# Global attention: the row step of the score maxima moved one unit earlier, and the results evicted by ScalarE through the score banks and finished on GpSimd

## The reference, cut to what matters

```
h = _layernorm(x) * (1 + ca) + sa
q, k, v = 16 heads of 8 features each, of h            # 4 sequences x 1024 tokens
scores = einsum('bhqd,bhkd->bhqk', q, k) / sqrt(8)
attn = softmax(scores, axis=-1)                        # needs the row maximum and the row sum
out = einsum('bhqk,bhkd->bhqd', attn, v)
x = x + ga * (out @ Wo.T + bo)
```

## Time and profile before

| what | value |
|---|---|
| median of 3 runs | 3825.5 us (3819.56 to 3826.06) |
| profiled execution, its own time | 3821.91 us |
| its span | 3820.1 us |
| PE, DVE, ACT, POOL busy in the span | 96%, 84%, 75%, 63% |
| loop of global attention, first score to last weighing | 87.24 to 748.29 us |
| mean granted PE clock | 0.987 of 2.4 GHz |

### The profile page before, as it was taken

One profiled execution on the slowest core, in us unless ns is written; L12 is line 12 of the kernel. 1 busy time (PEld: TensorE's weight loads), 2 busy tenths in 40 slices (PEclk: granted clock), 3 DMA queues, 4 the chain that ended last, 5 costly groups with the idle time before them and its releaser, 6 DMA issues. The chain is left out here.

```text
span 3820.1 us, 161411 instructions
## 1 busy us (share of the span) xinstructions
PE 3661.5 (96%) x70604; PEld 2660.4 (70%) x70604; DVE 3217.1 (84%) x4678; ACT 2863.7 (75%) x5074; POOL 2397.6 (63%) x1986
## 2 busy tenths in 40 slices
PE   6999999959999999999999999999999999999997
PEld 2222222247888888888888888888888888888885
DVE  7999999668888888888888888888888888888884
ACT  3888888857777777777777777777777777777774
POOL 3100000077777777878777777778777777778783
PEclk8999999989999999999999999999999999999999
DMA  3110000034444344433444344444444443444432
GB/s 117 38 39 21 20 22 18 7 95 109 110 112 106 104 122 113 111 107 104 119 115 112 105 106 116 120 110 105 106 116 116 111 106 105 127 117 109 108 105 57
DMA packets 202568, 360.17 MB, mean 94 GB/s; under 512 B 35522, under 2 KB 74054, under 8 KB 201542
## 3 DMA queue, kind: packets, MB, share of 16 engines
q1 hardware_dynamic: 201802, 348.76, 34.3%
HBM read 236.73 MB, written 111.67 MB: 91 GB/s over the span
## 5 line engine op out<-in xcount | busy, mean ns | idle before, releaser
L1202 POOL TENSOR_TENSOR T<-T 128x1024 f32<-128x1024 f32 x384 | 909.2, 2380 | 25.9 <-DVE T L1681 25.1
L1220 POOL TENSOR_TENSOR T<-T,rn 128x1024 f32<-128x1024 f32 x384 | 732.0, 1907 | 27.1 <-POOL rn L1213 0.4
L1292 PE MATMUL PA<-Wqkv,XS 128*128 128x512 f32 x2304 | 633.4, 410 | 11.4 <-DVE XS L1642 8.2
L787 ACT ACTIVATE E<-p_low 128x512 f32<-128x512 f32 x1024 | 556.2, 597 | 114.6 <-PE p_low L637 100.5
L716 DVE TENSOR_REDUCE negmax<-p_max 128x1 f32<-128x1024 f32 x512 | 588.9, 1215 | 19.7 <-PE p_max L616 19.7
L1292 PEld LDWEIGHTS PA<-Wqkv,XS 128*128 128x128 f32 x2304 | 414.7, 193 | 81.9 <-DVE XS L1642 11.2
L1689 DVE TENSOR_REDUCE ss<-SQ 128x32 f32<-128x2048 f32 x192 | 436.9, 2275 | 0.0
L1368 PE MATMUL PB<-ET,VW 64*64 64x32 f32 x24576 | 399.6, 220 | 16.8 <-DVE T L1681 8.8
L1368 PEld LDWEIGHTS PB<-ET,VW 64*64 64x64 f32 x24576 | 377.5, 135 | 54.8 <-DVE T L1681 28.6
L1320 PE MATMUL PD<-ident,T 128*128 128x128 f32 x3072 | 409.5, 276 | 6.3 <-POOL T L1220 5.3
L1381 PEld LDWEIGHTS PD<-Wo,OT 128*128 128x128 f32 x3072 | 365.9, 192 | 61.3 <-issue 61.1
(11 more groups left out here) (165 smaller groups left out, 6718.8 us busy)
## 6 DMA issues: line engine op xcount, KB each, us to landing
VW<-v_rows SPq DMA_DIRECT2D x768, 256.0 KB, 4.5
v_rows<-Vs SPq DMA_DIRECT2D x192, 512.0 KB, 6.0
Wraw<-in_Wqkv SPq DMA_DIRECT2D x40, 192.0 KB, 5.1
QA<-parts_q SPq DMA_DIRECT2D x384, 16.0 KB
KA<-parts_k SPq DMA_DIRECT2D x192, 32.0 KB
parts_q<-AO SPq DMA_DIRECT2D x8, 384.0 KB, 2.7
parts_k<-AO SPq DMA_DIRECT2D x8, 384.0 KB, 3.3
Wo<-in_Wo SPq DMA_DIRECT2D x12, 256.0 KB, 4.8
```

Of the source, the lines that this page charges most:

```text
L787: act.activation(E[:, s % 4, c, :], p_s[:, (64 * g + i) % NS, :], ACT.Exp, scale=DH ** -0.5)\
L1202: pool.tensor_tensor(out=t_, in0=t_, in1=T2[:, i * HALF:(i + 1) * HALF], op=ALU.add).then_inc(ad.sem, 1)
L1220: pool.tensor_tensor(out=t_, in0=t_, in1=rn[:, p, i * LH:(i + 1) * LH].unsqueeze(2).broadcast_to([P, LH, LD]), op=ALU.mult).then_inc(no.se ...
L1292: mm = pe.matmul(pair[:, half, :], XS[:, b, i, 1:P + 1], Wqkv[:, l % 2, j, lo:lo + 512], start=(k == 0), stop=(k == 2))
```

## The change

The row step moves from step 5 (and 13) to step 4 (and 12). It now stands between the two units of that step, behind the first unit of the next half, and the late order is gone: all steps have the same order. For this the units stand two earlier in the steps, and 8 instead of 6 of the first group's second half are done ahead of the loop. The PE transpose of the row step waits for the 16th unit of its half, two turns back, and no longer for the turn just before it.

The transposed results go to the next bank of the score ring instead of to `p_max`. ACT copies them out of it into `OE`, in its order among the exponentials, and POOL takes the reciprocals (a power of -1) and the products. `ring` numbers scores and results together. ACT's next copy of `p_o` into the same half of `OE` waits for POOL's product (`s_ao`).

```
-        if s < 5:
-            return [(g, 1, 6 + 2 * s + i) for i in range(2)]
+        if s < 4:
+            return [(g, 1, 8 + 2 * s + i) for i in range(2)]
...
-        return [(0, 0, i) for i in range(HU)], [(0, 1, i) for i in range(6)]
+        return [(0, 0, i) for i in range(HU)], [(0, 1, i) for i in range(8)]
...
+    def ring():
+        at = {}
+        def add(kind, *key):
+            at[(kind, *key)] = len(at)
+        for g in range(NG):
+            for s in range(16):
+                add("score", g, s, 0)
...
                 if s == 3 and g > 0:
                     add("result", g - 1, 1)
                 if s == 11:
...
     def on_pool(pool):
+        def result(g, qh):
+            b, hg = divmod(g, HG)
+            o = OE[:, qh, :].rearrange("p (q c w) -> p q c w", q=4, w=VW)
+            pool.wait_ge(s_ex.sem, s_ex.at(RING["result", g, qh]))
+            pool.tensor_tensor(out=rsum[:, qh, :, :], in0=o[:, :, :, DH], in1=minus[:, :, :], op=ALU.pow)\
+                .then_inc(s_rc.sem, 1)
+            pool.wait_ge(s_rc.sem, s_rc.at(g, qh + 1))
...
+            pool.tensor_tensor(out=a[:, :, hg, :, :], in0=o[:, :, :, 0:DH],
+                               in1=rsum[:, qh, :, :].unsqueeze(3).broadcast_to([P, 4, GH, DH]),
+                               op=ALU.mult).then_inc(s_ao.sem, 1)
...
             pool.tensor_copy(VG[:, g % 2, :, :, 0:DH + 1], VA[:, g // HG, :, heads(g), :]).then_inc(s_vg.sem, 1)
+            if g >= 2:
+                result(g - 2, 1)
+            if g >= 1:
+                result(g - 1, 0)
...
     def on_pe(pe):
...
         def max_rows(g, qh):
             k = TURN["rows", g, qh]
-            pe.wait_ge(s_mr.sem, s_mr.at(k - 1))
+            pe.wait_ge(s_mr.sem, s_mr.at(TURN["unit", g, qh, HU - 1]))
+            pe.wait_ge(s_mr.sem, s_mr.at(k - 2))
...
         def result(g, qh):
-            k = TURN["result", g, qh]
+            n = RING["result", g, qh]
             pe.wait_ge(s_oe.sem, s_oe.at(g, qh + 1))
-            pe.wait_ge(s_mr.sem, s_mr.at(k - 2))
+            pe.wait_ge(s_ex.sem, s_ex.at(n - NS))
             for qt in range(4):
-                mm = pe.transpose(p_max[:, k % 2, qt * P:(qt + 1) * P], OE[:, qh, qt * P:(qt + 1) * P], ident[:, :])
-            mm.then_inc(s_mx.sem, 1)
+                mm = pe.transpose(p_s[:, n % NS, qt * P:(qt + 1) * P], OE[:, qh, qt * P:(qt + 1) * P], ident[:, :])
+            mm.then_inc(s_st.sem, 1)
...
     def on_act(act):
...
             if g > 0:
-                act.wait_ge(s_mx.sem, s_mx.at(TURN["result", g - 1, qh]))
+                act.wait_ge(s_ao.sem, s_ao.at(g - 1, qh + 1))
             act.activation(OE[:, qh, :], p_o, ACT.Copy).then_inc(s_oe.sem, 1)
...
+        def result(g, qh):
+            n = RING["result", g, qh]
+            act.wait_ge(s_st.sem, s_st.at(n))
+            act.activation(OE[:, qh, :], p_s[:, n % NS, :], ACT.Copy).then_inc(s_ex.sem, 1)
```

More of the change, by code:

```diff
@@ L475, in global_attention @@
     s_md = m.count("s_md", 128)
-    s_st = m.count("s_st", 64)
-    s_ex = m.count("s_ex", 64)
+    s_st = m.count("s_st")
+    s_ex = m.count("s_ex")
+    s_ao = m.count("s_ao", 2)
+    s_mi = m.count("s_mi")
     s_pv = m.count("s_pv", 16)
@@ L523, in turns @@
                 todo = units(g, s)
-                late = s % 8 == 5
-                if todo and not late:
+                if todo:
                     add("unit", *todo[0])
-                if s == 5:
+                if s == 4:
                     add("rows", g, 1)
-                if s == 13 and g + 1 < NG:
+                if s == 12 and g + 1 < NG:
                     add("rows", g + 1, 0)
                 if todo:
-                    add("unit", *todo[0 if late else 1])
-                if todo and late:
                     add("unit", *todo[1])
+        return at
+    TURN = turns()
+    def ring():
[5 more added lines that the diff above has]
+                add("score", g, s, 0)
+                add("score", g, s, 1)
+                add("score", g, s, 2)
+                add("score", g, s, 3)
                 if s == 3 and g > 0:
@@ L540, in turns @@
         return at
-    TURN = turns()
+    RING = ring()
     def on_sp(sp):
@@ L601, in on_pool @@
                     .then_inc(w["l_w0s"].sem, 1)
+        result(NG - 2, 1)
+        result(NG - 1, 0)
+        result(NG - 1, 1)
         pool.wait_ge(s_gb.sem, NT + 1)
@@ L728, in max_rows @@
                               op=ALU.subtract).then_inc(s_mr.sem, 1)
[L730 to L740, removed]
-            a = AO[:, b, 4 * qh:4 * qh + 4, :].rearrange("p q (g c d) -> p q g c d", g=HG, d=DH)
-            dve.tensor_tensor(out=a[:, :, hg, :, :], in0=o[:, :, :, 0:DH],
-                              in1=rsum[:, qh, :, :].unsqueeze(3).broadcast_to([P, 4, GH, DH]),
-                              op=ALU.mult).then_inc(s_mr.sem, 1)
         before, after = begun_with(0)
@@ L792, in on_act @@
                         result_copy(g, 0)
+                if s == 3 and g > 0:
+                    result(g - 1, 1)
+                if s == 11:
+                    result(g, 0)
                 if s == 13 and 2 <= g < 5:
```

50 lines of the change are left out of this document (22 added, 28 removed).

## The result

The changed kernel takes 3797.7 us (median of 5 runs, 3796.6 to 3802.2), the kernel before 3822.8 us (5 runs, 3810.4 to 3826.1). The ratio is 0.9941, with a 95% interval of 0.9923 to 0.9959: 0.6% faster. In microseconds the ratio is 22.6 less, between 16 and 29; the two medians are 25.1 apart. The forecast was 3793, with a range of 3776 to 3811. The profiled execution of the changed kernel took 3802.2 us, the slowest of the five, so the traces are compared by stage and not by their spans (3820.1 and 3800.4 us).

What follows compares the result with a forecast made beforehand. The prediction took DVE's operations and its waits for PE to bound the loop. It summed -36.3 - 0.9 + 2.3 + 4.1 + 1.8 = -29.0 us on 3821.9, forecasting 3793 us, range 3776 to 3811.

Steps and rivals of the forecast that it cites:

- What bounds the loop: Even part of the loop: DVE's operations and its waits for PE make the time, 20.67 us a period.
- The result leaves DVE: At each result: 0.45 us of idle DVE replaces 0.78 us, so 0.33 us a period is gained.
- The row step: At the moved row step: 1.69 us beside the reductions becomes 0.78, so 0.91 us a period is gained.
- The wide weighing: Where PE weighs 512 queries and needs the copy of `p_o`: less slack, about 0.03 us late a period.
- The copies of the weights: ACT's three copies at the end of step 13: 0.6 us of DVE's time each, +1.8 us, between 0 and 3.
- The loop's end: Behind the last transposes: ACT's copy and POOL's power and product stand exposed, +4.1 us, between 1.7 and 5.2.
- What follows the loop is untouched: Stages behind the loop, from 3070 us: taken as equal before and after the change.
- The start: Ahead of the loop: two more units at half the clock, one loop step losing its units, +2.3 us.
- half a gain: Rival, 13%: at the row step PE comes late, half of the 0.91 us stays lost; 3807 us.
- The gap at the transposes isn't there: Rival, 12%: PE is ahead enough that no idle stands at the transposes; periods of 18.83 us, 3774 in all.
- ACT as the bound: Rival, 4%: at the ring PE waits in full for both ACT copies of a period; slower, 3832 us.
- that last rival: Rival, 3%: POOL's power holds ACT's copy in every group, no difference; the gain used up at about 19.5 us.

Runs made afterwards that it cites:

- e2: The changed kernel with the row step's late order and unit positions as before, so only the result leaves DVE; 3815.0 us, ratio 0.9997 to the kernel before.
- e1: The kernel before with only the row step moved as in the change, results staying on DVE; 3799.1 us, ratio 0.9954 to the kernel before.
- e4: The changed kernel with POOL's power taken twice for each result, the first into a spare tile; 3806.4 us (one run).
- e3: The changed kernel with a result's transposes, ring place and ACT copy moved into the next step, beside the row step; 3780.7 us, ratio 0.9909 to the kernel before.
- e7: The changed kernel with one more ACT copy of 128x512 into a spare tile ahead of each result's copy; 3796.1 us (one run).
- e8: The changed kernel with transposes beside the row step, last result on DVE, and ACT's weights copy in two halves; 3778.0 us, ratio 0.9900 to the kernel before.
- e5: The changed kernel with the very last result taken by DVE instead of ACT and POOL; 3792.7 us, ratio 0.9928 to the kernel before.
- e9: The changed kernel again, unaltered; 3790.2 us, ratio 0.9931 to the kernel before.
- e6: The changed kernel with the transposes beside the row step and the last result on DVE; 3782.9 us, ratio 0.9900 to the kernel before.

## Why the prediction was right, and where its terms were off

- **What bounds the loop: right.** DVE's reductions stand 1.131 us apart in the changed kernel as before. In the even part of the loop every gain and loss was one in DVE's chain, by its own work or by a fill that came late. Outside it, in the first period and behind the last units, it is the clock and the other engines that count.
- **The result leaves DVE: right, 0.03 us too little.** 0.78 us became 0.48 where 0.45 was counted (DVE begins the unit behind the transposes 1.61 us after the one before it, and the pace is 1.131). e2 shows 0.32 us gained against 0.33 counted. That DVE then waits for PE is what kept 0.57 us of removed work from being 0.57 us of gain.
- **The row step: right.** 1.69 us became 0.79, with 0.20 us of idle time where 0.15 was counted. e1 shows 0.80 us of the period for it, the 0.90 less what is lost at the wide weighing (next point).
- **The wide weighing: mis-sized.** I gave it 0.13 us of the period; DVE shows 0.18 (two reductions 1.315 us apart). ACT, and PE in order of time:

```profile
312.42 0.59 ACT L794 ACTIVATE OE<-p_low 128x512 f32<-128x512 f32 x1
312.52 0.39 PE L659 MATMUL p_max<-KA,QA 48*128 48x512 bf16 x1 [0.18 <-DVE negmax L756]
313.16 1.07 PE L697 MATMUL p_low<-E,VG 128*32 128x512 f32 x8
```

ACT's copy of `p_o` ends at 313.01 and the wide weighing, which needs it, begins at 313.16, 0.64 us behind the unit's fill (312.52); before, it was 0.54 (319.35 to 319.89). That the copy is the cause is read from this order and was not tested; in e4, where the copy comes 2.2 us late, the weighing does follow it. These 0.05 us, 0.03 at the result, 0.02 at the row step and 0.01 for each reduction behind one that waited (1.14 and not 1.131) make 19.58 of 19.46 us. The gain is 1.09 and not 1.21 us a period, **32.8 and not 36.3 us**.
- **The copies of the weights: right.** Three periods are 20.18 us, 0.60 more than the others, as counted. The reason is only in part the one given. That the late order's slack had hidden them is right: e2 keeps it and loses nothing, e1 drops it and loses 0.60. That PE has just been held up by the transposes is not what makes it cost 0.60, for in e3 the transposes cost DVE nothing (periods of 19.09 us) and the copy still costs 0.60. By e7 and e8 the length of ACT's hold, 1.0 us, is what counts: 0.48 us cost nothing at the result, and two halves together 0.23. Between length and place of the hold no run decides alone.
- **The loop's end: right, 3.5 us for 4.1.** The power took 2.91 us. My 3.5 was a choice between 1.1 and 4.6, so that it came near is in part luck; the product took 0.41 as worked out from POOL's multiplies. With the 4.3 us of its other work POOL's pair in groups 3 to 5 is done 0.6 us ahead of ACT's copy (212.68 to 213.32), and e4 shows the wait as soon as that is used up.
- **Left out: the clock behind the loop.** "What follows the loop is untouched" was wrong by 1.4 us. PE's idle time went from 0.95 to 4.44 us, and the next stage began at half the clock and took 1.4 us longer. In e5, with 0.93 us of idle time, both are gone.
- **The start: 2 us too little.** The first score comes 2.5 us later, near the 2.35 counted. The first period, from the first cast to the second, took 22.94 us where 20.9 was to be expected (21.75 before, less 0.91 for the row step, 0.1 more for two units at the pace ahead of the loop). The clock rose later in this execution: from 95 to 98 us it was still at half, where before it was whole from 95 on. e9, the same program, had 0.68 in that window:

```profile
95.00:98.00 3.00, 3.00 (x22) 0.41 (x16) 1.69 (x2) 1.10 (x3) 0.00 (x0) 0.68 0.02 5
```

Nine traces (the changed kernel, e1, e3 to e9) have the same work in this period, and it is the longer the later the clock rises: 22.05 us in e9, where it rises 15.9 us after the first cast, 22.94 in the changed kernel (17.8) and 24.80 in e8 (22.2), or 0.43 us for each microsecond. Before, it rose after 14.2 us. By an estimate from these figures the clock is some 1.5 of the 2.0 us; the other 0.5 stay open.

The terms as measured are -32.8 in the periods, +1.8 at the copies and +3.5 at the end. The next stage begins 24.4 us earlier, which leaves +3.1 for the start and all else; I had +1.4 for it, 2.3 less the 0.9 of group 0. The 1.7 us between them are the first period, less 0.4 us that the shorter last one gives back. With +1.4 behind the loop the sum is -23.0. The runs say -22.6 by the ratio and -25 by the medians, with an interval of -16 to -29. My sum was -29.0. The main error is 3.5 us in a term of 36.3; then come 1.7 us at the start, mostly the clock, 1.4 us behind the loop, which are the clock, and 0.6 us the other way at the end.

Of the rivals, "half a gain" fell: the transposes hold PE up just ahead of the row step, and still its transpose is done 0.43 us ahead of the cast (320.28 + 0.28 and 320.99), so the row step took 0.79 us for 0.78. "The gap at the transposes isn't there" was wrong for this kernel, and is what e3 then made: 19.09 us a period, where DVE's work, the 0.20 behind the row step and the weighing are all that is left beside 18.10. ACT as the bound fell with e7, POOL with e4. (In that last rival I left out what such a power costs at the loop's end, about 15 us; with it the gain is used up at about 19.1 us and not at 19.5.)

On the rule of the Trainium skill's "GPSIMD Engine Reference", section 4.1, that elementwise work is better on VectorE, this case's traces agree in the direction: the product took 0.41 us on POOL and 0.29 on DVE, 1.4 times and not twice, and the reciprocal 2.91 as a power against 0.25. In the loop this cost nothing, as POOL was idle, and at the end, where nothing hides it, it cost the 3.5 us and with the clock 4.9; there the rule holds, and e5's trace is 5.0 us better for following it.

The better kernel than both is e6 or e8, 1.0% faster than the kernel before, where the change gave 0.6 to 0.7%.

## What to carry to other kernels

Work that is taken off the engine that sets the pace gives back only what the next fill doesn't turn into waiting. Before the work's own length, count when the next fill can start and how long it takes until the engine can begin on it, here 0.64 us. If an in-order engine must do something besides, put it where it waits for a buffer anyway; moving four transposes by half a step gave 14 us where the whole change had given 24. What is hidden in a loop isn't hidden in its last turn, and a slow engine there also let PE's clock fall for the stage behind. Compare stages and not whole runs when the gain is of the size of the scatter in stages that nobody touched, here 15 us.

## What the runs showed of the hardware

- After 4.44 us in which PE did nothing the clock was granted at 1.2 GHz for the 4 us from 726.2 on, and the following stage took 1.4 us longer; after 0.93 us it stayed at 2.4 GHz. The fall to 1.2 GHz stands in all six traces in which POOL makes the last result (4.4 to 7.3 us idle, the stage 0.9 us longer in e3 and 1.3 to 1.4 in the others), and in none of the other five.
- After 2.5 us of idle PE the clock fell in two of three cases, all in e4; where it fell, the period lost 3.8 us, and 2.3 where it stayed whole.
- The moment at which the clock first rises at the loop's start isn't fixed: with the same work ahead of it, it came 17.8 us after the first cast in one execution of the changed kernel and 15.9 in another (first periods of 22.94 and 22.05 us), and 17.1 and 22.2 in e6 and e8, which don't differ there (22.62 and 24.80 us). Once at 2.4 GHz, periods of the same work repeat to a hundredth of a microsecond.
- A power on POOL took 2.91 us for 128x16 and 1.02 for 128x4. By an estimate from these two that is 0.16 us for each element of a partition and some 0.4 us besides. With the power taken twice the loop's end came 2.9 us later (e4). A multiply of 128x128 took 0.41.
- ACT instructions of 128x512 start 0.48 us apart when nothing is waited for (312.42, 312.90, 313.37 and 313.85 in the changed kernel), though the row of each says 0.59 or more.
